# Rounded weights made inside the delta rule, scores of the attention in rounded parts, and a narrower last level

## What is computed

```python
x = x + delta_rule(_layernorm(x))   # 8 heads of 128, 2 updates of the state per row
x = x + ffn(_layernorm(x))          # 256 -> 512 -> 512 -> 256, relu
x = x + attention(_layernorm(x))    # 16 query heads in 4 groups, bias and mask
x = x + ffn(_layernorm(x))
```

```python
state = state * exp(g_t)
for j in range(2):
    corr = k_j @ state
    state = state + outer(k_j, (v_j - corr) * b_j)
o_t = q_t @ state
```

## Time and profile before

| what | us |
| --- | --- |
| median of 3 runs | 4883.27 |
| the profiled execution's own time | 4879.77 |
| span of the profiled execution | 4878.0 |
| tables, 0 to 165 | 165 |
| delta rule, 165 to 2785 | 2620 |
| first feed-forward, 2785 to 3155 | 370 |
| attention, 3155 to 4660 | 1505 |
| second feed-forward, 4660 to 4878 | 218 |

### The profile page before, as it was taken

How to read it: one execution, slowest core, us unless ns; L and a number is a source line. 1 busy time by engine, 2 the same in 40 slices (tenths; PEclk the granted TensorE clock), 3 DMA queues, 4 the chain that set the end, 5 groups by cost and what they waited for, 6 DMA issues and landing times. The chain is left out here.

```text
span 4878.0 us, 87441 instructions
## 1 busy us (share of the span) xinstructions
PE 4470.0 (92%) x27647; PEld 3678.8 (75%) x27647; DVE 2889.1 (59%) x7476; ACT 2192.6 (45%) x5668; POOL 1173.2 (24%) x2691
## 2 busy tenths in 40 slices
PE   3599999999999999999999689789999999999979
PEld 3488888888888888888888578656666666666668
DVE  5566666666666666666666345255555555555545
ACT  2344555555555455555555234244444444444434
POOL 5233443433433344434343000000000000000000
PEclk9999999999999999999999699799999999999989
DMA  7333333333333333333333232211111111111011
GB/s 265 129 93 95 98 91 100 92 96 114 96 100 91 95 100 91 100 91 92 106 106 93 70 105 78 73 43 47 34 43 34 47 43 34 47 43 29 23 58 35
DMA packets 558410, 392.49 MB, mean 80 GB/s; under 512 B 253040, under 2 KB 504944, under 8 KB 556400
## 3 DMA queue, kind: packets, MB, share of 16 engines
q1 hardware_dynamic: 557936, 386.69, 25.7%
HBM read 288.36 MB, written 98.14 MB: 79 GB/s over the span
## 5 line engine op out<-in xcount | busy, mean ns | idle before, releaser
L928 DVE SCALAR_TENSOR_TENSOR g_conv<-g_r,g_taps,g_conv 128x511 f32<-128x511 f32 (+2 forms) x961 | 702.9, 742 | 152.9 <-ACT g_conv L813 131.5
L817 ACT ACTIVATE g_us<-g_chn 128x128 f32<-128x128 f32 x528 | 146.1, 277 | 744.7 <-PE g_chn L629 743.8
L593 PE MATMUL g_lev<-g_nu,g_T 128*128 128x128 f32 (+1 forms) x3120 | 432.3, 279 | 0.8 <-DVE g_nu L940 0.8
L1954 ACT ACTIVATE a_pr<-a_pr,a_low 128x128 f32<-128x128 f32 (+3 forms) x512 | 286.9, 561 | 313.3 <-DVE a_low L2096 309.4
L593 PEld LDWEIGHTS g_lev<-g_nu,g_T 128*128 128x128 f32 (+1 forms) x3120 | 379.4, 177 | 33.5 <-issue 11.8
L1744 PE MATMUL a_sc<-a_kT,a_qT 128*128 128x128 f32 (+3 forms) x1024 | 340.3, 459 | 60.6 <-DVE a_low L2096 55.9
L1108 POOL TENSOR_TENSOR g_prod<-g_small 64x14 f32<-64x14 f32 (+6 forms) x896 | 227.0, 253 | 685.9 <-DMA g_small<-lower_d 620.7
L2227 POOL TENSOR_TENSOR a_bias<-a_kb,a_start 128x128 f32<-128x128 f32 (+2 forms) x96 | 56.5, 617 | 1380.1 <-DVE a_low L2096 938.3
L562 PE MATMUL g_r<-g_x_hi,g_w_hi 128*128 128x512 f32 x770 | 358.8, 466 | 7.2 <-issue 4.0
L2096 DVE CUSTOM_DVE_ANT_0 a_pr<-a_sc,a_bias 128x128 f32<-128x128 f32 (+3 forms) x512 | 244.5, 486 | 193.9 <-issue 187.9
L586 PE MATMUL g_lev<-g_U,g_L 128*128 128x128 f32 x2340 | 332.6, 278 | 0.0
(11 more groups left out here) (347 smaller groups left out, 11353.3 us busy)
## 6 DMA issues: line engine op xcount, KB each, us to landing
g_w_hi<-ws_d SPq DMA_DIRECT2D x65, 768.0 KB, 5.6
g_w_lo<-ws_d SPq DMA_DIRECT2D x65, 768.0 KB, 6.8
lower_d<-g_L SPq DMA_DIRECT2D x64, 512.0 KB, 3.2
g_T<-low_d SPq DMA_DIRECT2D x64, 512.0 KB, 4.1
g_U<-upp_d SPq DMA_DIRECT2D x64, 512.0 KB, 5.3
a_w<-w_groups SPq DMA_DIRECT2D x32, 640.0 KB, 4.6
oT_d<-g_oT SPq DMA_DIRECT2D x67, 256.0 KB, 5.1
f_oT<-oT_d SPq DMA_DIRECT2D x8, 2048.0 KB, 9.1
```

The source lines that it names most:

```text
L593: mm = M.matmul(lev[hf][0:rows, c, :].rearrange("p (j n) -> p j n", j=2), T[0:rows, hf * HC + c, 0:rows], nu[0:rows, hf * HC + c, :].unsqu ...
L928: ins = V.scalar_tensor_tensor(out=y[:, k:L], in0=x[:, 0:L - k], scalar=tap, in1=y[:, k:L], op0=ALU.mult, op1=ALU.add)
L1954: A(pr[g % 2][:, i, 0:width(i)], pr[g % 2][:, i, 0:width(i)], ACT.Exp, scale=-1.0, bias=low[g % 2][:, i:i + 1], accum_out=tot[g % 2][:, i: ...
```

## The change

1. The table stage no longer loads, splits or stores the head weights; `ws_d` goes. In the delta rule SP loads the raw weights of a unit in one DMA (`weights`), later in its turn; the taps have a load of their own. ScalarE rounds them to hi in two halves (`split_w`, k = 0 and 1) and VectorE subtracts to get lo, both in the middle of the turn before.
2. In the last level, chunks past the first of a half use 64 moving columns, in `lev_nu` and in `lev_un`.
3. Attention: scores as three fp32r products from hi and lo of query and key; ScalarE makes the hi of each, VectorE the lo. Score tiles go in pairs, (0, 1) and (2, 3), with the next query's projection between. The marks go through GpSimd (`diagonals`) and one fp32r matmul of a matrix of ones with 384 columns, VectorE multiplies the result with the tail sums (`tl`), and `head_out`, now on VectorE, adds `tl` to the output; the two tail matmuls per head go. `tail_rows` makes columns instead of rows. The key's projection comes before the job for the next batch.

The diff, cut to its core (the start and end of each stage, which do the same once, are left out, as are semaphore names):

```diff
 # tables
-            def split_head(h, pair, par):
-                nc.gpsimd.tensor_tensor(wh_hi[par][:], wh[par][:], ones, ALU.mult)
-                nc.gpsimd.tensor_tensor(wh_lo[par][:], wh[par][:], wh_hi[par][:], ALU.subtract)
-                store_head(b, par)
-                if more or par == 0:
-                    load_head(b + 2, par)
 # delta rule, SP
-            def weights(h, par):
-                for i, piece in enumerate((w_hi, w_lo)):
-                    sp.dma_start(piece[par][:]..., io["ws_d"][bass.ds(h, 1), i:i + 1]...)
-                sp.dma_start(taps[par][:], ...)
+            def weights(h):
+                sp.dma_start(w_raw[:], io["w_heads"][h % H]).then_inc(s["d_wr"], 16)
+            def tap_rows(h, par):
+                sp.dma_start(taps[par][:], io["taps"][h % H]).then_inc(s[f"d_w{par}"], 16)
...
-                sp.wait_ge(s["d_proj"], NB * u + 1)
                 sp.wait_ge(s["d_conv"], 5 * u + 1)
-                weights(hp * QN + q + 1, 1 - par)
+                tap_rows(hp * QN + q + 1, 1 - par)
...
                     sp.dma_start(blocks_of(name), inv[:, i]).then_inc(s["d_XT"], 16)
+                sp.wait_ge(s["d_wlo"], KD * u + 2 * KD)
+                weights(hp * QN + q + 2)
                 sp.wait_ge(s["d_un"], NL2 * u + NL2)
 # TensorE
-                        mm = M.matmul(lev[hf][0:C, c, :], Lm[o][C:P, hf * HC + c, 0:C], U[o][C:P, hf * HC + c, :], start=True, stop=True)
+                        mm = M.matmul(lev[hf][0:C, c, C:P], Lm[o][C:P, hf * HC + c, 0:C], U[o][C:P, hf * HC + c, C:P], start=True, stop=True)
...
+                    if li == NLV - 1 and c:
+                        mm = M.matmul(lev[hf][0:C, c, 0:C], T[0:C, hf * HC + c, 0:C], nu[0:C, hf * HC + c, :], start=True, stop=True)
+                        continue
...
-                    pe.wait_ge(s[f"d_w{1 - par}"], 48 * (pair + par) + 48)
+                    pe.wait_ge(s["d_wlo"], KD * u + 2 * KD)
                     pe.wait_ge(s["d_at"], u + 2)
                     project(u + 1, 1 - par, K0)
 # ScalarE
                     A(gate[q][:], BANK[GB][:], ACT.Silu).then_inc(s["d_gate"], 1)
+                    split_w(u + 1, 1 - par, 0)
                 copy_u(u, 5)
                 if own:
                     silu(u, q, V1)
+                    split_w(u + 1, 1 - par, 1)
                     act.wait_ge(s["d_L"], 2 * u + 4)
                     decay_end(u + 1)
                 copy_u(u, 6)
...
+            def split_w(u, par, k):
+                act.wait_ge(s["d_wr"], 16 * u + 16)
+                act.wait_ge(s["d_proj"], NB * (u - 1) + 1)
+                A(w_hi[par][:, k], w_raw[:, k], ACT.Copy).then_inc(s["d_whi"], 1)
 # VectorE
+            def split_w(u, par, k):
+                dve.wait_ge(s["d_whi"], KD * u + k + 1)
+                V.tensor_tensor(w_lo[par][:, k], w_raw[:, k], w_hi[par][:, k], ALU.subtract).then_inc(s["d_wlo"], 1)
...
                     lev_add(u, o, 0, 1)
+                if own:
+                    split_w(u + 1, 1 - par, 0)
                 chain_S(u, q, 6)
...
                     lev_mask(u, 1, 1)
+                if own:
+                    split_w(u + 1, 1 - par, 1)
+                if inverse:
                     lev_add(u, o, 1, 0)
 # attention, TensorE
-                    M.matmul(sc[i % 2][:, 0:width(i)], qT[g % 2][:, i * P:(i + 1) * P], kT[tp_][:, 0:width(i)], start=True, stop=True).then_inc(s["sc"], 1)
+                    product(sc[i % 2][:, 0:width(i)], [(q_hi[g % 2][:, at], q_lo[g % 2][:, at], k_hi[tp_][:, 0:width(i)], k_lo[tp_][:, 0:width(i)])]).then_inc(s["sc"], 1)
...
-                for i in range(TAIL):
-                    mm = M.transpose(pb[0:TAIL, i * P:(i + 1) * P], fl[:, i, :], ident)
+                M.matmul(pb[:, 0:TAIL * P], ones[:], dg[:].rearrange("p i n -> p (i n)"), start=True, stop=True).then_inc(s["ftr"], 1)
...
-                M.matmul(out[:, 0:TAIL * P], vt_hi[:, at], frow[:], start=False, stop=False)
-                M.matmul(out[:, 0:TAIL * P], vt_lo[:, at], frow[:], start=False, stop=True).then_inc(s["pv"], 1)
...
-                for m in range(1, TT):
-                    mm = M.matmul(pb[0:TAIL, :], cc["tails"][:, m * TAIL:(m + 1) * TAIL], v[bp][:, m, :], start=(m == 1), stop=(m == TT - 1))
+                for n in range(HKV):
+                    for m in range(1, TT):
+                        mm = M.matmul(pb[:, TAIL * P + n * TAIL:TAIL * P + (n + 1) * TAIL], v[bp][:, m, n * P:(n + 1) * P],
+                                      cc["tails"][:, m * TAIL:(m + 1) * TAIL], start=(m == 1), stop=(m == TT - 1))
...
-                scores(t, 2, here)
+                scores(t, 2, here, (0, 1))
                 if nxt:
                     pe.wait_ge(s["kT"], t + 2)
                 query(t, here, bp, 3)
+                scores(t, 2, here, (2, 3))
 # ScalarE
+            def query(t, g):
+                act.wait_ge(s["q"], G * t + g + 1)
+                A(q_hi[g % 2][:], pa[:], ACT.Copy).then_inc(s["q_hi"], 1)
...
-                head_out(t, here, 0)
 # VectorE
-                V.tensor_copy(qT[g % 2][:], pa[:]).then_inc(s["qT"], 1)
+                V.tensor_tensor(q_lo[g % 2][:], pa[:], q_hi[g % 2][:], ALU.subtract).then_inc(s["qT"], 1)
+            def key(t, tp_):
+                V.tensor_tensor(k_lo[tp_][:], pa[:], k_hi[tp_][:], ALU.subtract).then_inc(s["kT"], 1)
...
-                V.tensor_copy(frow[:], pb[0:TAIL, 0:TAIL * P]).then_inc(s["frow"], 1)
+                V.tensor_tensor(tl[tp_][:, 0:TAIL * P]..., pb[:, 0:TAIL * P]..., vtT[:, n, :]..., ALU.mult).then_inc(s["frow"], 1)
+            def head_out(t, tp_, g):
+                dve.wait_ge(s["pv"], G * t + g + 1)
+                V.tensor_tensor(oT[tp_][:, g, :], out[:], tl[tp_][:], ALU.add).then_inc(s["oT"], 1)
...
                 normalise(t, 2)
+                head_out(t, here, 0)
 # GpSimd
+            def diagonals(t):
+                pool.wait_ge(s["fl"], t + 1)
+                Gp.tensor_tensor(dg[:], ident..., fl[:]..., ALU.mult).then_inc(s["dg"], 1)
```

More of the change, by code:

```diff
@@ L1832, in turn @@
                     key(t + 1, there, nb)
-                scores(t, 2, here)
+                if n and more:
+                    pe.wait_ge(s["frow"], t + 1)
+                if n == 1 and more:
+                    pe.wait_ge(s["xn"], b + 2)
+                    columns_of(0, pb)
+                elif n == 2 and more:
+                    gate_rows(1 - bp)
+                elif n == 3 and more:
+                    value_rows(1 - bp, 2)
+                scores(t, 2, here, (0, 1))
                 if nxt:
@@ L1854, in turn @@
                     project_out(t - 1, there, 0)
-                scores(t, 3, here)
+                scores(t, 3, here, (0, 1))
                 if nxt:
@@ L1858, in turn @@
                     query(t + 1, there, nb, 0)
+                scores(t, 3, here, (2, 3))
                 turn_probs(t, 2)
@@ L1909, in _ @@
             query(0, 0, 0, 1)
-            scores(0, 0, 0, True)
+            scores(0, 0, 0, range(TT), True)
             loop(pe, turn)
@@ L1969, in turn @@
                 nxt = more or n < HKV - 1
-                exps(t, 1)
+                exps(t, 1, (0, 1))
+                query(t, 2)
+                exps(t, 1, (2, 3))
                 evac(t, 0)
-                if not begin:
-                    head_out(t - 1, there, 3)
-                if n == 0:
-                    tail_rows(b)
-                elif n == 1 and more:
+                if nxt:
+                    key(t + 1, there)
+                if n == 1 and more:
                     columns(b + 1, 1 - bp, 0, pb)
@@ L1996, in turn @@
                 if nxt:
[L1997 removed]
+                    exps(t + 1, 0, (0, 1))
+                    query(t + 1, 1)
+                    exps(t + 1, 0, (2, 3))
                 evac(t, 3)
[L1999 removed]
                 if n == 1 and more:
@@ L2136, in turn @@
                 normalise(t, 1)
-                flag_rows(t)
+                if not begin:
+                    head_out(t - 1, there, 3)
                 if n == 0:
                     tail_rows(b)
-                elif n == 1 and more:
+                flag_rows(t, b, n, here)
+                if nxt:
+                    diagonal(t + 1, there, (n + 1) % HKV, nb, kb_count(b, bp, n))
+                    key(t + 1, there)
+                if n == 1 and more:
                     columns(b + 1, 1 - bp, 0, pb)
@@ L2203, in _ @@
             gate_end(0)
+            key(0, 0)
             query(0, 0)
@@ L2218, in _ @@
             Gp.memset(eps[:], LN_EPS)
-            Gp.memset(fl[:], 0.0)
+            for t in tl:
+                Gp.memset(t[:], 0.0)
+            Gp.memset(one[:], 1.0)
             Gp.memset(start[:], 0.0).then_inc(s["init"], 1)
```

170 lines of the change are left out of this document (77 added, 93 removed).

## The result

The changed kernel takes 4640.04 us (median of 4 runs, 4636.3 to 4642.76) against 4885.12 (median of 4 runs) of the kernel before in the runs beside it: ratio 0.9499, interval 0.9482 to 0.9515, 245 us faster. The forecast was 4682, the range 4630 to 4738.

The account below looks back on a forecast made before the run. TensorE was taken to bound the delta rule and the attention. From the profiled 4879.8 us, -26 (tables), -12 (delta rule) and -163 (attention) give 4678.8; with 3.5 for the median of runs, 4682, range 4630 to 4738.

Parts of the forecast that it names:

- rival 3: Delta rule: the second ScalarE copy is absorbed, so the stage gains 43 us more, 4639 in all; chance 0.08.
- Tables, -26: Table stage: without GpSimd's splitting, VectorE's operations on x stay at 1.76 us and the last xT copy starts earlier: -26 us.
- Delta rule, -12: Delta rule, per unit: +0.67 for ScalarE's second copy, -0.17 and -0.69 for the narrow last level; over 64 units -12 us.
- Attention, -163: Attention, 32 turns of 4 heads: tails, scores, flags, waits and lateness sum to -173, clock +10, giving -163 us.
- Tails -82: Attention: dropping two tail matmuls per head saves 0.64 us for each of 128 heads, -82 us.
- Scores -31: Attention: three f32r products per head take 1.91 us instead of 2.15 in fp32, -31 us over 128 heads.
- rival 1: Attention scores: f32r at width 128 costs as much as fp32, +42 us, 4724 in all; chance 0.15.
- Flags -30: Attention: one f32r product replaces three transposes and their wait, saving 0.95 us per turn, -30 us over 32 turns.
- Waits -48, and +18 behind them: Attention: the third score tile's wait for VectorE goes, -48 us; late key low part and first logits add +18.
- Clock +10: Attention: tail_rows' 3-column matmuls may bring a second fall of TensorE's clock per batch; a third of 8 x 3.3 us, +10.
- Rival 2: Attention: VectorE becomes the bound through 3.1 us more work per turn, +45 us, 4727 in all; chance 0.17.
- The rival on the other side: Delta rule: doubled wait at chunk 6 lowers TensorE's clock once per unit, costing 211 us, 4893 in all; chance 0.03.

Follow-up runs that it names:

- experiment 4: Changed kernel with ScalarE's second rounding copy moved up, right behind the first and ahead of the copy of u for chunk 5: 4595.27 us, ratio 0.9404 to the kernel before.
- Experiment 3: Kernel before, with GpSimd no longer splitting the head weights in the table stage, all loads and stores kept: 4855.4 us, ratio 0.9938.
- experiment 1: Kernel before with only the last level's matmuls narrowed to 64 moving columns: 4832.21 us against 4884.96, ratio 0.9890.
- experiment 7: Kernel before without the two tail matmuls per head and the wait ahead of them: 4796.29 us against 4882.85, ratio 0.9820.
- experiment 5: Changed kernel with scores as one fp32 matmul instead of three fp32r products: 4678.2 us, ratio 0.9581 to the kernel before.
- experiment 11: Kernel before with only the next query's matmuls moved between score tiles 1 and 2 of a head: 4824.71 us, ratio 0.9881.
- experiment 6: Changed kernel with a head's four score tiles made one after the other and the next query behind them again: 4742.4 us, ratio 0.9712 to the kernel before.
- experiment 2: Kernel before with the whole attention stage of the changed kernel, tables and delta rule as before: 4687.4 us, ratio 0.9600.

## Why the prediction was right, and where it was off

**The number.** The measured 4640.04 lies inside the stated range, 4630 to 4738, but outside the forecast's own range of 4645 to 4715. It falls on the 4639 of rival 3, and that is chance: rival 3 had ScalarE's second copy absorbed, and experiment 4 shows that it cost 0.7 us per unit. The prediction called its lower end "half-way to rival 3"; half-way is 4660, and 4630 lies beyond rival 3. With the end where the words put it the measurement would have been outside. So the mechanisms were right in the main, and that the range held owes something to luck.

**Tables, -26: right.** Experiment 3 confirms the cause and the size (-29.6), and the start of the last copy was met within 0.3 us.

**Delta rule, -12: right in its terms, -17 measured.** The last level's saving was put at 0.86 per unit, -55; alone it gave -52.8. The rounding copy on ScalarE was put at +0.67 per unit, +43; moving it away gave back 44.8, and TensorE's wait had grown by 45.9. The two sum to -8. The stage gave 9 more.

The 9 are not an effect of the ScalarE stall: the wait for `g_at` is 29.1 us in experiment 1, 14.9 in the changed kernel, and 14.2 in experiment 4, where the stall is gone. What differs is where GpSimd stands. First lines of experiment 1 (a timeline, then a group in ns min/median/max), then of the changed kernel:

```profile
1880.86 0.72 POOL L1115 TENSOR_TENSOR g_prod<-g_small,g_const 64x256 f32<-64x256 f32 x1
1880.89 0.72 DVE L1048 TENSOR_TENSOR g_bk<-g_rk,g_tab 128x8 f32<-128x8 f32 x1
...
L1045 DVE SCALAR_TENSOR_TENSOR g_oden<-g_oss,g_qden x66: 161/163/730, 224.3 to 2728.0; 128x4 f32<-128x4 f32 x66
```

```profile
1527.19 0.21 DVE L1041 TENSOR_TENSOR g_bk<-g_rk,g_tab 128x8 f32<-128x8 f32 x1
...
1528.03 0.72 POOL L1110 TENSOR_TENSOR g_prod<-g_small,g_const 64x256 f32<-64x256 f32 x1
...
L1038 DVE SCALAR_TENSOR_TENSOR g_oden<-g_oss,g_qden x66: 161/164/215, 197.0 to 2735.7; 128x4 f32<-128x4 f32 x66
```

VectorE makes two small tiles, `g_oden` and `g_bk`, on its way to `g_at`. In experiment 1 one of the two takes about 0.7 us instead of 0.16 in 30 of the 64 units, beside GpSimd's 0.72 us, and the projection waits 0.69 us on average in those and 0.25 in the other 34. In the changed kernel GpSimd comes to that operation later, neither tile takes over 0.22 us in any unit, and all 64 waits are 0.23. Thirty times 0.44 is 13 us, enough for the 9. The traces show this unit by unit; no run changes it alone, and the delta rule of the kernel before itself took 2616.4 to 2622.1 us in five executions.

The likely reason why GpSimd comes later stands in the same trace, and the forecast had not priced it: VectorE's two subtractions cost TensorE nothing that shows, but they hold up GpSimd's substitution, which runs beside them. GpSimd's operation starts 0.1 us behind the start of `g_oden` in experiment 1, 0.9 in the changed kernel and 1.6 in experiment 4 (medians). The timeline of GpSimd in the changed kernel, while VectorE's subtraction (L959 of that kernel) runs from 1517.85 for 0.95 us:

```profile
1517.61 0.23 POOL L1106 TENSOR_TENSOR g_prod<-g_small 64x26 f32<-64x26 f32 x1
1517.91 0.99 POOL L1108 TENSOR_TENSOR g_small<-g_small,g_prod 64x26 f32<-64x26 f32 x1
1518.99 0.24 POOL L1106 TENSOR_TENSOR g_prod<-g_small 64x36 f32<-64x36 f32 x1
```

The operation at 1517.91 takes 0.99 us where its neighbours take 0.24. GpSimd so loses some 1.4 us per unit over the stage, and no entry of TensorE's list of waits comes from it. The Trainium skill (SBUF — State Buffer, Who interferes with whom) says that a VectorE instruction with two SBUF inputs contends with a GpSimd one that reads SBUF, and that the second to issue blocks until the first ends; the trace agrees, 0.99 against 0.24 us, and shows VectorE, the first, undelayed.

**Attention, -163: 33 us too little.** By terms, the first number as put:
- Tails -82: -87 (experiment 7).
- Scores -31: -34 to -38 (experiment 5). The bound that mattered, width 128 at 0.11 us, held, so rival 1 is out.
- Flags -30: the frow waits of 20.5 us are gone, and the section from the marks to the key is one product of 0.26 us. Not tested alone.
- Waits -48, and +18 behind them: the term that was most mis-sized. The list of waits counts one only from the modelled end of the matmul ahead. From start to start, over 31 turns, the third tile's waits were 68 us in the kernel before, where the list has 48, and are 20 in the changed kernel. With the 7.0 on the key's low part that is -41 for the whole term, where the forecast had -30: 11 of the 33. Its weight is shown from both sides: alone the reordering gave -57.8 (experiment 11), and in the changed kernel it holds off 102 us (experiment 6).
- Clock +10: the step that failed. It was right that the new 3-column matmuls of tail_rows bring falls: in 3 of 8 batches the clock falls within 1.5 us behind them, for 1.7 us of loss each. The forecast left the other falls where they were, but they moved too: the gate turns lost 18.8 us before and 13.7 after. Over the 31 turns the stretches at half clock cost 20.5 us before and 20.5 after, so the term was 0: 10 of the 33. It also changes from one execution to the next; the same stage lost 15.4 us in experiment 2.
- Rival 2, VectorE as the bound, is out as long as the query stands between the tiles: VectorE is busy 907.9 of 1351 us, 67% up from 53%, and TensorE's waits for it shrank. Experiment 6 shows how near it is: with the same work in another order it cost 102 us.

Tails, scores, waits and clock explain 29 to 33 of the 33 us. The sum is rough, for the experiments on single terms start from different kernels.

**The rival on the other side** (the wait at chunk 6 doubling to 1.3 us and a fall of the clock in every unit) had its first half come true: the wait is 1.35 us in the unit shown above, and 91.1 us over 76 waits. The fall did not follow: over the 2602 us of the delta rule the clock is 0.99, as before. In the attention, experiment 6 shows waits lowering the clock, at 17 us over 31 turns, 0.55 each where the rival had 3.3 per unit.

## What to carry to other kernels

When a tile waits for another engine's answer in the same pair of banks, put independent matmuls between the second tile and the third before making the matmuls cheaper; the cheaper they are, the more that order is worth. When an operation is moved into a unit, look at which idle time of its engine ends on nothing: the same copy cost 0.7 us per unit behind V1's silu and nothing that could be measured 5.5 us earlier. And where the longest of a group of equal VectorE or GpSimd operations is far above its median and no wait is shown, look at what the other of the two engines does beside it.

## What was not expected of the hardware

- Short waits cost more than they last: in experiment 6, 76 us of added waiting, spread over the heads, came with some 15 us of slower matmuls; the stretches at half the clock cost 37.6 us instead of 20.5.
- Filling up matmuls kept the clock: 24 of 128 columns, 0.11 us apart, were followed by 1.00 in all seven gate turns; 24 of 8 columns, as far apart and in the same place, were followed by a fall to half in five of seven.
- Instructions with 64 rows of weights and 64 moving columns stand 0.058 us apart, those with 128 moving columns 0.109, but a change between the 64-row and the 128-row form costs some 0.1 us more at each end. So a group of 6 fell by 0.31, from 0.80 to 0.49, and not by half; the forecast had taken 0.35.
- VectorE and GpSimd hold each other up for whole instructions: an operation on x took up to 3.46 us instead of 0.41 beside GpSimd's operations of 3.42 us, GpSimd's 0.24 us became 0.99 beside VectorE's 0.95, and even an operation on 8 columns went from 0.16 to 0.72 us beside GpSimd's 0.72.
